# A one-layer ViT block with a routed feed-forward stage: five token tiles for projection, norm and router, transposes two steps behind the scores, front and drain reordered

## The reference

```python
h = patchify(x) @ W_tok + b_tok                       # 768 -> 192
q, k, v = split(h @ w_qkv.T)                          # 12 heads of 64
q, k = (t * rsqrt(norm(t, axis=heads) + 1e-8) for t in (q, k))
p = softmax(q @ k.T / scale[head])                    # 36 x 36, within one image
h1 = layernorm(h + (p @ v) @ w_out.T + b_out)
logits = h1 @ Wr + br                                 # 8 experts
top, idx = top_k(logits, 2); w = softmax(top)
gu = min(h1 @ Wgu[e] + bgu[e], 7); gate, up = gu[:192], max(gu[192:], -7)
act = (up + 1) * gate * sigmoid(1.702 * gate)
ffn = sum over the two chosen e of w_e * (act @ Wd[e] + bd[e])
out = layernorm(h1 + ffn)
```

## Time and profile before

| | us |
|---|---|
| median of 3 runs | 178.46 |
| lowest and highest | 177.28, 178.48 |
| the profiled execution's own time | 177.54 |
| its span, first to last instruction | 175.8 |
| outside the span (177.54 - 175.8) | 1.7 |

### The profile page before, as it was taken

How to read it: one execution, slowest core, us unless ns; L and a number is a source line. 1 busy time by engine, 2 the same in 40 slices (tenths; PEclk the granted TensorE clock), 3 DMA queues, 4 the chain that set the end, 5 groups by cost and what they waited for, 6 DMA issues and landing times. The chain is left out here.

```text
span 175.8 us, 3428 instructions
## 1 busy us (share of the span) xinstructions
PE 154.2 (88%) x1234; PEld 138.1 (79%) x1234; DVE 116.7 (66%) x278; ACT 92.5 (53%) x192; POOL 96.5 (55%) x100
## 2 busy tenths in 40 slices
PE   6999998998799598599999799789989999999840
PEld 2689797997687486588878698579979999999830
DVE  0399799949869567349684726297576665688642
ACT  3465994372776447217888755433546346333500
POOL 7891196399336895956879791045333334444101
PEclk9999999999999999799999879999999999999995
DMA  5999986200600033020000000000000000000101
GB/s 157 345 320 240 279 221 181 80 0 4 175 6 2 6 89 89 4 80 9 4 0 0 4 2 0 4 0 0 2 4 0 0 0 6 0 0 4 50 0 50
DMA packets 4400, 10.62 MB, mean 60 GB/s; under 512 B 608, under 2 KB 1312, under 8 KB 4384
## 3 DMA queue, kind: packets, MB, share of 16 engines
q1 hardware_dynamic: 4384, 10.41, 20.7%
HBM read 9.96 MB, written 0.44 MB: 59 GB/s over the span
## 5 line engine op out<-in xcount | busy, mean ns | idle before, releaser
L362 POOL TENSOR_TENSOR reg_r<-reg_q,reg_r 128x288 fp32r<-128x288 f32 x22 | 18.2, 828 | 25.8 <-ACT reg_r L572 25.8
L311 POOL TENSOR_TENSOR reg_w<-stage,reg_w 128x768 fp32r<-128x768 f32 x12 | 23.5, 1971 | 7.5 <-ACT reg_w L416 7.5
L572 ACT ACTIVATE reg_r<-reg_q 128x288 fp32r<-128x288 f32 x24 | 10.7, 444 | 29.6 <-DVE reg_q L877 29.6
L340 POOL TENSOR_TENSOR reg_p<-reg_p,rinv 108x648 f32<-108x648 f32 (+1 forms) x12 | 15.0, 1252 | 10.6 <-DVE rinv L781 10.6
L856 DVE TENSOR_SCALAR reg_q<-ps,bup 128x288 f32<-128x288 f32 x24 | 12.4, 517 | 8.7 <-PE ps L1056 8.6
L1220 PE MATMUL ps<-wout,oT 128*108 128x192 f32 (+1 forms) x72 | 15.3, 371 | 1.0 <-DVE w2T L847 1.0
L1052 PE MATMUL ps<-reg_r,reg_w 128*128 128x288 f32 x48 | 15.0, 312 | 0.0
L1220 PEld LDWEIGHTS ps<-wout,oT 128*108 128x108 f32 (+1 forms) x72 | 13.2, 195 | 2.0 <-issue 1.2
L1056 PE MATMUL ps<-reg_r,reg_w 128*128 128x288 f32 x48 | 14.2, 295 | 0.0
L1053 PE MATMUL ps<-reg_r,reg_w 128*128 128x288 f32 x48 | 14.1, 295 | 0.0
L1055 PE MATMUL ps<-reg_r,reg_w 128*128 128x288 f32 x48 | 14.1, 294 | 0.0
(11 more groups left out here) (197 smaller groups left out, 484.8 us busy)
## 6 DMA issues: line engine op xcount, KB each, us to landing
reg_x<-xw_in SPq DMA_DIRECT2D x6, 416.0 KB, 6.2
stage<-w_gu_a SPq DMA_DIRECT2D x4, 384.0 KB, 4.7
stage<-w_gu_b SPq DMA_DIRECT2D x8, 192.0 KB, 3.7
stage<-w_qkv_a SPq DMA_DIRECT2D x3, 384.0 KB, 10.2
stage<-w_qkv_b SPq DMA_DIRECT2D x6, 192.0 KB, 10.1
stage<-w_down SPq DMA_DIRECT2D x3, 384.0 KB, 3.4
wout<-w_out SPq DMA_DIRECT2D x1, 576.0 KB, 12.9
out<-reg_q SPq DMA_DIRECT2D x6, 72.0 KB, 1.7
```

Source lines behind the costliest of these rows:

```text
L311: nc.gpsimd.tensor_tensor(dst[:, 1, :], raw, f(dst[:, 0, :]), ALU.subtract).then_inc(s_wlop, 1)
L340: nc.gpsimd.tensor_tensor(pp, pp, rinv[0:n, u % 2, :].unsqueeze(2).to_broadcast([n, 6, n]), ALU.mult).then_inc(s_p, 1)
L362: nc.gpsimd.tensor_tensor(acts[:, n % NACT, 1], act_f[:, n % 4], f(acts[:, n % NACT, 0]), ALU.subtract).then_inc(s_alo, 1)
```

## The change

**Tiles.** Attention keeps its six groups. What follows it (projection, norm, transposes, router) runs on five tiles, `TSIZES` = 108, 108, 108, 124, 128. Tile 3 needs O of groups 3 and 4, tile 4 of groups 4 and 5; for groups 3 to 5, O goes into the space of the used K. `w_transpose` and what follows it run twice, for tiles 0 to 2 and for 3 and 4, in place of six times.

**Two steps behind.** PE's step k now has `p_transpose(k-2)` and `weighted(k-3)`, with a third buffer `Pr2`; ACT's evacuations move with them. `ln1_stats` opens DVE's odd steps and `ln1` comes after `sum_recip`. `project(0)` to `(2)` come in steps 4, 6, 8; `project(3)` and `(4)` in the drain.

**Front.** ACT loads the table for the root early (`warm`), takes `root(0)` before `square(10)`, and evacuates V 0 to 2; DVE takes V 3 to 5 and the last two sums of K squares. POOL's `w_lo(6)` and `(7)` wait until DVE has scaled Q and K of group 0.

```diff
+TSIZES = [GRP, GRP, GRP, 124, 128]
+LATE = 3
...
+        Pr2 = sb("Pr2", [128, 6 * GRP])
...
+        filler = reg_h[:, 0:BANK // 2].bitcast(bf16)
...
@@ POOL
-            for m in range(7, 12):
+            for m in range(7, 10):
                 add_square(m)
...
+            pool.wait_ge(s_qn, 1)
             w_lo(6)
+            pool.wait_ge(s_kn0, 1)
             w_lo(7)
             k_norm(1)
             for k in range(0, NU):
-                if k >= 4 and k % 2 == 0:
-                    root(k // 2 - 2, SIZES[k // 2 - 2], s_ve, s_rstd)
+                if k in (5, 7, 9):
+                    root(k // 2 - 2, TSIZES[k // 2 - 2], s_ve, s_rstd)
                 probs(k)
...
-                if k >= 7:
+                if 7 <= k < 11:
                     w_lo(k + 4)
+            root(3, TSIZES[3], s_ve, s_rstd)
+            w_lo(15)
+            act_lo(0)
             w_lo(16)
...
@@ ACT
+            nc.scalar.activation(warm[:, :], sm[:, C_SCALE:C_SCALE + 1], ACT.Sqrt)
             act.wait_ge(s_const, 1)
+            root(0)
             square(10)
-            root(0)
             square(11)
             first_root(0)
+            v_evac(0)
+            v_evac(1)
             root(1)
             first_root(1)
+            v_evac(2)
...
-            v_evac(4)
...
             for k in range(0, NU):
                 exps(k)
+                if k == 10:
+                    h1_evac(2)
+                if k >= 3:
+                    o_evac(k - 3)
                 if k >= 2:
-                    o_evac(k - 2)
-                if k >= 1:
-                    pt_evac(k - 1)
+                    pt_evac(k - 2)
...
+                if k in (8, 11):
+                    choose((k - 8) // 3)
...
+            o_evac(9)
+            pt_evac(10)
+            choose(2)
+            expert(0)
             o_evac(10)
             pt_evac(11)
...
@@ DVE
             for k in range(0, NU):
-                if k >= 4 and k % 2 == 0:
+                if k in (5, 7, 9):
                     ln1_stats(k // 2 - 2)
                 if k + 1 < NU:
                     row_max(k + 1)
-                if k >= 4 and k % 2 == 0:
-                    ln1(k // 2 - 2)
                 if k in (1, 3, 5, 7):
                     q_norm(k // 2 + 2)
                 sum_recip(k)
+                if k in (5, 7, 9):
+                    ln1(k // 2 - 2)
...
@@ PE
                 if k == 0:
                     v_proj(5)
-                if k in (9, 11):
-                    w_transpose(k // 2 - 4)
+                if k == 10:
+                    h1_transpose(2)
+                if k == 11:
+                    logits(2)
+                    gate_up(0)
+                if k >= 3:
+                    weighted(k - 3)
                 if k >= 2:
-                    weighted(k - 2)
-                if k >= 1:
-                    p_transpose(k - 1)
-                if k >= 6 and k % 2 == 0:
+                    p_transpose(k - 2)
+                if k in (6, 8):
+                    h1_transpose(k // 2 - 3)
+                if k in (4, 6, 8):
+                    project(k // 2 - 2)
+                if k in (7, 9):
                     logits(k // 2 - 3)
...
+            gate_up(1)
+            weighted(9)
+            p_transpose(10)
+            project(3)
             weighted(10)
             p_transpose(11)
-            gate_up(0)
-            logits(3)
-            gate_up(1)
+            gate_up(2)
             weighted(11)
-            h1_transpose(4)
-            gate_up(2)
-            w_transpose(2)
-            project(5)
+            h1_transpose(3)
+            w_transpose(0)
+            gate_up(3)
             spread(0)
-            gate_up(3)
+            residual(0)
             spread(1)
-            residual(0)
+            project(4)
             spread(2)
-            h1_transpose(5)
+            down(0)
             gate_up(4)
...
```

More of the change, by code:

```diff
@@ L150, in two, with probabilities, o_tiles, o_stationary @@
             return ap.rearrange("p (a n) -> p a n", a=2)
+        def probabilities(u):
+            return (Pr[:, 0], Pr[:, 1], Pr2)[u % 3]
+        def o_tiles(g):
+            if g < LATE:
+                return oT[:, g % 2, :, 0:SIZES[g]]
+            o = OFFS[g] - OFFS[LATE]
+            return qk[:, NP:2 * NP, o:o + SIZES[g]]
+        def o_stationary(i, m):
+            if i < LATE:
+                return oT[:, i % 2, m, 0:TSIZES[i]]
+            o = TOFFS[i] - TOFFS[LATE]
+            return qk[:, NP + m, o:o + TSIZES[i]]
+        W_BATCH = [(0, 1, 2), (3, 4)]
         s_x = [sem(f"s_x{i}") for i in range(NC)]
@@ L269, in _ @@
         def _(pool):
-            nc.gpsimd.memset(filler[:, :], 0.0).then_inc(s_filler, 1)
+            nc.gpsimd.memset(filler, 0.0).then_inc(s_filler, 1)
             for t, value in ((ident[:, :], 0.0), (fold[:, :], 0.0), (onehot_f, 0.0), (mask_lf, 0.0),
-                             (half[:, :], -0.5), (euler[:, :], math.e), (w2[:, :], 0.0), (mask_rf, MASKED)):
+                             (half[:, :], -0.5), (euler[:, :], math.e), (w2[:, :, :], 0.0), (mask_rf, MASKED)):
                 nc.gpsimd.memset(t, value).then_inc(s_fill, 1)
@@ L377, in _ @@
                     w_lo(8 + k // 2)
-                if k >= 7:
+                if 7 <= k < 11:
                     w_lo(k + 4)
+            root(3, TSIZES[3], s_ve, s_rstd)
+            w_lo(15)
+            act_lo(0)
             w_lo(16)
[L381 to L384, removed]
             act_lo(1)
             act_lo(2)
+            root(4, TSIZES[4], s_ve, s_rstd)
             act_lo(3)
-            gap_exp(4)
             act_lo(4)
             act_lo(5)
-            gap_exp(5)
-            for n in range(6, LAST_LO):
+            act_lo(6)
+            gap_exp(3)
+            gap_exp(4)
+            for n in range(7, LAST_LO):
                 act_lo(n)
@@ L626, in _ @@
             expert(5)
+            h1_evac(4)
             act_hi(4)
@@ L642, in _ @@
                 act_hi(n if n >= NT + 4 else n - 1)
-                if n == 10:
-                    w2_hi(5)
+                if n == 9:
+                    choose(4)
+                if n == 11:
+                    w2_hi(1)
                 if n == NT + 2:
@@ L962, in _ @@
             expert_act(2)
-            h1_lo(5)
+            ln1_stats(4)
             up_in(4)
+            ln1(4)
             weigh(3)
             expert_act(3)
-            read_logits(4)
-            rank(4)
             up_in(5)
@@ L976, in _ @@
             expert_act(5)
-            w2_lo(3)
-            rank(5)
             up_in(7)
@@ L981, in _ @@
             expert_act(6)
-            router_weights(5)
+            read_logits(3)
+            rank(3)
+            read_logits(4)
             up_in(8)
@@ L985, in _ @@
             expert_act(7)
-            w2_lo(4)
+            router_weights(3)
+            rank(4)
             for n in range(9, 2 * NT):
@@ L1023, in keep_warm @@
                 for _ in range(n):
-                    mm(ps[:, 3, :], filler[:, 0:128], filler[:, :], start=True, stop=True)
+                    mm(ps[:, 3, :], filler[:, 0:128], filler, start=True, stop=True)
             pe.wait_ge(s_filler, 1)
@@ L1409, in _ @@
             down(4)
-            w_transpose(4)
             gate_up(9)
@@ L1421, in _ @@
                 spread(n - 1 if n < NT + 4 else n)
-                if n == 10:
-                    w_transpose(5)
+                if n == 11:
+                    w_transpose(1)
                 if n < NT + 3:
```

254 lines of the change are left out of this document (123 added, 131 removed).

## The result

The kernel after takes 167.33 us (median of 4 runs, 166.11 to 167.83), the kernel before 178.47 (4 runs, 177.28 to 178.51): a ratio of 0.938, interval 0.931 to 0.945. The forecast was 167.0. The profiled execution of after took 167.69 us with a span of 165.2 (before: 177.54 and 175.8).

A forecast was written before the change was run, and what follows sets the result against it. PE bounds the experts; attention and drain lose 14.6 us to waits and half clock. Start -1.6, stage -10.5, behind `spread(2)` +0.3 and +0.5 give -11.3: from the median 178.46 to 167.2, predicted 167.0, range 163.0 to 173.5.

The forecast's parts named there:

- The start: Front before the first scores: ACT's copy of V 2 beside DVE's scaling of K starts scores 1.6 us earlier.
- (a): Steps 1 and 2: `row_max(2)` late on DVE, `q_norm(2)` meeting POOL's `k_norm(2)`; two waits of about 1.5, 3.0 us.
- as no single wait of my list is over 1.5 us: Attention stage on PE: with only such waits left, both half-clock projections (3.22 and 4.10 us, not 2.29) go.
- Rival D: One slow stretch only remains, a projection and its neighbours, +2 us: 169; counted within the forecast's 0.52.
- The transpose two steps behind has more than a whole step of slack, so the 2.50 wait falls.: Attention on PE: over 2.5 us of slack for exps, sum and POOL removes the 2.50 us wait for probabilities.
- The ledger: PE, first score to `spread(2)`: work 55.0 us before, 51.9 after; waits and half clock 14.6 before, waits 7.2 after.
- (b): Step 6: `h1_transpose(0)` waits 0.7 us for `ln1(0)`, whose root stands behind `probs(4)` and `k_norm(4)` on POOL.
- (d): Drain: `project(3)` waits for `o_evac(9)`, `gate_up(2)` for the first gelu, `w_transpose(0)` for `o_evac(11)`; 1.2 us.
- (c): Steps 9 to 11: the chain of tile 2 with only the short group beside it costs 1.0 us of waits.
- A: Rival: POOL becomes the bound from `probs(0)` to `gap_exp(2)`; four more meetings with DVE, 5 us: 172.0; chance 0.25.
- B: Rival: shorter drain, or the waits of (a) absent; PE's waits fall to about 4 us: 163.8; chance 0.13.
- C: Rival: clock falls in steps 1 to 3, PE runs at half; not faster, up to 187 us; chance 0.03.

The follow-up runs named there:

- e4: Kernel after with the front of the kernel before put back; 167.20 us (167.07 to 167.65).
- e6: Kernel after with the six products of `project(4)` issued twice, as one more projection; 167.89 us (167.18 to 169.40).
- e1: Kernel before with only `ln1` moved behind `sum_recip` on DVE in even steps; 171.86 us against 178.19, ratio 0.968.
- e5: Kernel after with transposes, weighted sums, norm and router steps one step earlier, a lag of one; 172.41 us (167.95 to 174.91).
- e3: Kernel before with only the new front of the kernel after; 175.74 us against 178.19.
- e11: The lag-of-one kernel e5 with `choose(1)` one step earlier on ACT, at step 10; 169.49 us (167.12 to 173.28).
- e8: Kernel after with `choose(1)` on ACT at step 10 and not 11; 166.66 us (165.78 to 167.66).
- e7: Kernel after with eight filler matmuls, results unused, before `subtract_max(2)` and `subtract_max(3)` on PE; 166.23 us (166.10 to 168.24).
- e2: Kernel after with `ln1` put back ahead of `sum_recip` on DVE in steps 5, 7 and 9; 171.71 us (169.42 to 172.79).
- e10: The lag-of-one kernel e5 with eight and two filler matmuls ahead of `p_transpose` in steps 2 and 3; 172.43 us (170.64 to 173.50).

## Why the prediction was right, and where it was not

The total was right to 0.3 us. The steps under it were not all right, and that closeness is in part luck. The stage gave 8.7 us where 10.5 were forecast; the start gave 0.5 more and what lies behind `spread(2)` cost 0.6 less, so that the span fell by 10.6 and not 11.3. The profiled execution, forecast at 166.2, took 167.69.

**The start.** Forecast -1.6, the trace shows -2.07 (45.28 against 47.35). But e4 shows that in the kernel after it is worth only 1.0 us at full clock, since DVE and POOL have not caught up at steps 2 and 3, and nothing in the median, since the clock then falls in half of the executions. The prediction took it at its full size.

**The waits, (a).** Forecast two waits of about 1.5 us together 3.0, measured 0.93 and 1.60, at the named places and for the named reason: `q_norm(2)` met `k_norm(2)` and took 2.06 us.

**The step that failed: "as no single wait of my list is over 1.5 us", the slow stretches fall.** In after's profile the clock fell behind 0.93 and 1.60 us with one short burst of work between them, and cost that step 1.56 us. No single wait was over 1.60, so the length of a single wait was the wrong sign to go by. e6's profile, with the same waits and no fall, and the executions at full clock show that the fall comes in some executions only; its price in the span is 0.8 us. Rival D had the mechanism, but put it at a projection and at +2. The milestones of after's profile: `subtract_max` 5, 7, 9 and 11 came at 66.53, 74.18, 82.47 and 88.07, in place of 65.0, 73.2, 81.3 and 86.7: late by 1.0 to 1.5 us from step 5 on and no later after it. In e6's profile, without the fall and counted from a first score at 45.28, they are 64.97, 73.42, 81.70 and 87.30: there the forecast holds within 0.6 us.

**"The transpose two steps behind has more than a whole step of slack, so the 2.50 wait falls."** It falls, but e1 shows that the order of `ln1` and the row sum takes it away with a lag of one. The prediction had named that order as the cause of the wait and then gave the cure to the lag. Near full clock the parts are: order -3.7 (174.98 to 171.3, e1), then front, tiles and drain -3.4 (to e5's 167.95, of which e3 gives the front 1.2), then the lag -1.7 (to 166.2). That is 8.8 us. The medians differ by 2.4 more, and this is clock: before loses 3.2 us to it (178.2 against 174.98), after 0.75. The tiles were never run alone; 2.2 for them and the drain is what is left of that sum. e5 is a single execution at that clock, and e11 against e8 gives the lag 0.6, so the lag is worth 0.6 to 1.7 us, and what it has less the term before it has more.

**The ledger.** Work after was taken as 51.9 us and waits as 7.2; the stage with full clock (e4) has PE busy 54.96 of 59.12, so work was 3 us too small and waits about 3 too large. The total of the stage was 59.1 forecast and 60.94 measured. Before, the same error had hidden in the 14.6 of "waits and half clock": e1's 57.66 us of busy PE stand against my 55.0. The difference, one projection and what moved, was right: 3.1 against 2.7.

**(b) to (d).** (b), the wait of `h1_transpose(0)`, is not in after, which is late there itself; it shows at 0.65 to 0.67 us in e4, e6 and e7, as forecast (0.7). (c): steps 9 to 11 took 88.07 - 82.47 = 5.60 us, forecast 5.4. (d) 1.2: 0.36 and 0.63 measured; the 4.04 us of `rank(2)` behind `choose(1)` was not seen.

**Behind `spread(2)`.** Forecast +0.8, measured +0.2. `rank(4)` waits 1.15 us for `choose(3)` as said, and `root(4)` is late as said.

**Rivals.** A, POOL as the bound: POOL is busy 19.80 of 22.91 us in the middle, and no transpose waits for it; wrong. B: wrong, the drain was as long as forecast. C: the fall that it feared came, but ended within a step. "Granted clock 1.00 from 47 on" and "`spread(2)` near 105" (106.22) did not hold; the 60 projection records and the dense PE in steps 5 to 9 did (7.65 to 8.29 us a pair).

**The rule of the SBUF ports.** The prediction set a row in which the one that began first lost against the Trainium skill (SBUF — State Buffer, "SBUF: two separate sides"). In after the meeting of step 2 goes by the rule: POOL began at 53.48 and took 1.56 us, DVE at 53.67 and took 2.06, more than twice its 0.83 at 49.63:

```profile
49.63 0.83 DVE L774 TENSOR_TENSOR reg_q<-reg_q,rnorm 128x648 f32<-128x648 f32 x1 [0.46 <-ACT rnorm L501]
...
53.48 1.56 POOL L362 TENSOR_TENSOR reg_q<-reg_q,rnorm 128x648 f32<-128x648 f32 x1
53.67 2.06 DVE L774 TENSOR_TENSOR reg_q<-reg_q,rnorm 128x648 f32<-128x648 f32 x1
```

By the rule DVE would end at 53.48 + 1.56 + 0.83 = 55.87, and it ended at 55.73. The next meeting of after agrees too: DVE began at 60.32 beside a multiplication of POOL from 59.76 to 61.03, and took 1.40. But the kernel before has a second row against it beside the earlier trace rows: POOL's `k_norm(5)` began at 82.04 and took 1.05 us, where it takes 0.65 in after at 74.99, and DVE's `q_norm(5)` began at 82.21 and took 0.37, as it does alone. So most meetings go by the rule and some do not. The prediction reckoned with the loss on DVE's side in (a), and it is there.

## What to carry to other kernels

Before giving a wait's end to a deeper pipeline, look at what stands ahead of its producer on that engine's list: here one swap of two operations was worth more than the third buffer (3.7 us against 0.6 to 1.7, at like clock), and about a fifth of the whole gain (2.4 of 11.2 us) came from a clock that falls less. An earlier start is worth only what the next chain behind it leaves (1.0 of 2.1 us here), so price it at the first point where the engines meet again. Waits found in the profile after (a 4 us stall on an engine "off the path", a queue entry ahead of a short one) add up: three small moves of order gave about 1.7 us more at full clock, and with the filler 2.4 in the median. A single profile is one execution: with the same list and the same waits one profile had the slow stretch and another had not, so a statement on the clock needs the executions counted.

## What was not expected of the hardware

Waits of 0.93 and 1.60 us with 2.1 us of work between them were followed by about 3 us at a granted clock of 0.50 in four profiles (after twice, e2, e8) and not in the fifth (e6). A wait of 1.95 us at 58 us was followed by such a stretch in e11 and not in e5 (1.96) or e1 (1.85). In e10 and e11 the clock fell behind a wait of 1.03 us at about 88 to 90 us, and in e5 it did not. What decides from one execution to the next stays open. The mean clock of an execution takes a few distinct values (before: 28 of 33 at 0.949, at 0.957 or 0.958, or at 0.966 to 0.968, and 2 at 0.991), and the time goes in steps with it: about 5 us between the first and the last. A median over such executions says how often the clock fell as much as how long the kernel is.
